# A decoder's last stage: gated squares in a new order, and identity products at four borders

## The reference

```python
shared = x2 @ sw1.T * _sqrelu(x2 @ swg.T) @ sw2.T      # x2: 2048 tokens x 256
xl = x2 @ Wdown.T                                       # 2048 x 64
...                                                     # w_dense: 2048 x 16, the gates, 8 of 16 not zero
for e in range(E):                                      # E = 16
    ye = xl @ rw1[e].T * _sqrelu(xl @ rwg[e].T) @ rw2[e].T
    acc = acc + w_dense[:, e:e + 1] * ye
out = shared + acc @ Wup.T
```

## Time and profile before

| what | value |
|---|---|
| median of 3 runs | 1069.51 us (1068.92 to 1071.56) |
| the profiled execution, its time | 1066.24 us |
| its span | 1064.5 us |
| mean granted clock | 0.977 |
| DVE, ACT, POOL busy | 778.5, 710.1, 303.4 us |
| last stage begins, experts' pairs begin, last of them ends | about 916.8, 949.7, 1047.25 us |

### The profile page before, as it was taken

How to read it: one execution, slowest core, us unless ns; L and a number is a source line. 1 busy time by engine, 2 the same in 40 slices (tenths; PEclk the granted TensorE clock), 3 DMA queues, 4 the chain that set the end, 5 groups by cost and what they waited for, 6 DMA issues and landing times. The chain is left out here.

```text
span 1064.5 us, 19092 instructions
## 1 busy us (share of the span) xinstructions
PE 999.2 (94%) x6751; PEld 830.1 (78%) x6751; DVE 778.5 (73%) x1541; ACT 710.1 (67%) x1961; POOL 303.4 (28%) x250
## 2 busy tenths in 40 slices
PE   7999999999999999999988867899998799799998
PEld 3888988988998898898987655677776699575555
DVE  5888868667676676766767888899887444567775
ACT  5888777767767777766743366678787244458882
POOL 1342333332332233333300110244454000103442
PEclk9999999999999999999999898899999899899999
DMA  7221000000000000000241000000000000024432
GB/s 214 85 61 59 2 1 1 2 1 1 1 1 2 1 23 14 1 1 2 80 123 22 1 1 1 1 2 2 2 2 2 2 1 2 16 66 121 101 99 80
DMA packets 31837, 31.79 MB, mean 30 GB/s; under 512 B 8192, under 2 KB 23296, under 8 KB 31744
## 3 DMA queue, kind: packets, MB, share of 16 engines
q1 hardware_dynamic: 31744, 30.59, 10.3%
...
## 5 line engine op out<-in xcount | busy, mean ns | idle before, releaser
L345 POOL TENSOR_TENSOR roped_q<-roped_q,sin_q 128x512 f32<-128x512 f32 x64 | 82.0, 1281 | 301.1 <-DVE sin_q L490 301.1
L1622 ACT ACTIVATE win_P<-banks,win_neg_max 128x128 f32<-128x128 f32 x256 | 91.3, 380 | 27.6 <-DVE win_neg_max L1696 26.8
L345 POOL TENSOR_TENSOR roped_k<-roped_k,sin_k 128x512 f32<-128x512 f32 x64 | 83.3, 1301 | 46.1 <-DVE sin_k L490 46.1
L399 ACT ACTIVATE P<-banks,neg_max 128x128 f32<-128x128 f32 x256 | 90.5, 372 | 5.8 <-DVE neg_max L515 5.6
L433 ACT ACTIVATE oT_hi<-banks,bv_col 128x512 fp32r<-128x512 f32 x64 | 44.1, 689 | 74.2 <-PE banks L663 74.2
L1578 POOL TENSOR_TENSOR win_P<-win_P,win_inv 128x512 f32<-128x512 f32 x64 | 66.9, 1046 | 72.9 <-DVE win_inv L1701 72.9
L408 ACT ACTIVATE sin_k<-banks 64x512 f32<-64x512 f32 x128 | 76.0, 594 | 11.0 <-PE banks L37 9.4
L518 DVE SCALAR_TENSOR_TENSOR oT_lo<-banks,bv_col,oT_hi 128x512 fp32r<-128x512 f32 x64 | 47.9, 749 | 42.6 <-ACT oT_hi L433 42.0
L408 ACT ACTIVATE sin_q<-banks 64x512 f32<-64x512 f32 x128 | 76.0, 594 | 2.9 <-PE banks L37 0.7
L625 PE MATMUL banks<-WO_lo,oT_hi 128*128 128x256 f32 x256 | 72.9, 285 | 0.0
L489 DVE SCALAR_TENSOR_TENSOR roped_k<-banks,qk_bias,cos 128x512 f32<-128x512 f32 x64 | 48.0, 750 | 32.6 <-ACT sin_k L408 32.6
...
## 6 DMA issues: line engine op xcount, KB each, us to landing
...
```

Source lines behind the costliest of these rows:

```text
L345: nc.gpsimd.tensor_tensor(roped[w][:, p, :], roped[w][:, p, :], sin_part[w][:], ALU.add).then_inc(roped_sum[w], 1)
L399: ins = nc.scalar.activation(P[:, i, :], SC[:, i * 128:(i + 1) * 128], ACT.Exp, bias=neg_max[:, r % 2, i:i + 1], accum_out=exp_sum[:, r % ...
L1622: ins = nc.scalar.activation(P[:, h % 2, s, i, :], SC[2 * (h % 2) + s][:, i * 128:(i + 1) * 128], ACT.Exp, bias=neg_max[:, h % 2, at:at + ...
```

## The change

In `phase_moe`:

- The latent is kept once, `XL_hi` and `XL_lo`, two groups in the two halves of the partitions (`split_latent`). `up_pair(n)` makes the gate products of two steps and then their up products: for each, three products of 64 rows (high x low, low x high, high x high) for either half in turn, into two banks. `U1` has four banks, `Y` two.
- ScalarE makes two relus, then two squares; `relu` and `squared` have four slots.
- The gates multiply the square, not the output of `down`: on GpSimd for three of four steps, on VectorE (`gate_here`) for the one with s % 4 == 1. `gate_of` holds all 2048 tokens of an expert on all 128 partitions, loaded in two halves of tokens.
- `down(n)` adds up over the experts in `Y[n % 2]` in PSUM and comes two pairs after its up product; `weigh` and the additions are gone. At the end ScalarE and VectorE copy the two sums to `acc`.
- `split_latent(3)` and `gate_hidden(0)` come after the gates, whose transpose on TensorE comes before the up product of step 2.

At four borders, `keep_busy(count)` and a loop add products of the identity with itself, 128 columns of float32, into a bank that nobody reads: 16 in the retention, 7 before the spline stage's transposes, 6 and 5 at the start of cross attention, 5 at its end, 5 and 2 in the last stage.

```diff
                 pe.wait_ge(gate_ready, 2 * PAIRS)
                 pe.wait_ge(w_split, 2)
+                def keep_busy(count):
+                    for _ in range(count):
+                        nc.tensor.matmul(WOB[0][:, 0:128], ident[:], ident[:], start=True, stop=True)
+                keep_busy(16)
                 for p in range(PAIRS + 1):
                     if p < PAIRS:
                         transpose_wy(p)
...
             def _(pe):
+                def keep_busy(count):
+                    for _ in range(count):
+                        nc.tensor.matmul(bank[4][:, 0:128], ident[:], ident[:], start=True, stop=True)
+                keep_busy(7)
...
+                def keep_busy(count):
+                    for _ in range(count):
+                        nc.tensor.matmul(OUT[:, 0:128], ident[:], ident[:], start=True, stop=True)
+                keep_busy(6)
                 transpose_x(0)
+                keep_busy(5)
                 project_q(0)
                 project_k(0)
                 transpose_x(1)
...
                     weigh(2 * i + 1)
+                for _ in range(5):
+                    nc.tensor.matmul(KB[:, 0:128], ident[:], ident[:], start=True, stop=True)
...
-        weighted = spare[:].rearrange("p b h n -> p (b h n)")[:, 0:3 * GW].rearrange("p (i n) -> p i n", i=3)
-        acc = spare[:].rearrange("p b h n -> p (b h n)")[:, 3 * GW:5 * GW].rearrange("p (i n) -> p i n", i=2)
+        acc = sb("moe_acc", [128, 2, GW])
...
-        UG, U1, Y = bank[0:2], bank[2:5], (bank[6], bank[7], bank[5])
-        up_bank = lambda s: Y[1] if s == 0 else U1[s % 3]
+        UG, U1, Y = bank[0:2], bank[2:6], bank[6:8]
+        up_bank = lambda s: Y[0] if s == 0 else U1[s % 4]
...
+        on_dve = lambda s: s % 4 == 1
+        gated_by_dve = lambda s: max(0, (s + 3) // 4 - 1)
+        gated_by_pool = lambda s: max(0, s + 1 - NG - gated_by_dve(s))
+        pair_done = lambda s: s + 1 if s < NG else NG + (s - NG) // 2 + 1
...
                     if e >= GATE_SLOTS:
-                        sp.wait_ge(weighted_done, 2 * (e - GATE_SLOTS) + 2)
-                    row = gate_rows[e].rearrange("(c h n) -> h c n", c=2, h=2)
-                    for half in range(2):
-                        src = row[half].rearrange("(a c) n -> a c n", a=1).broadcast_to([LAT, 2, GW])
-                        sp.dma_start(gate_of[half * LAT:(half + 1) * LAT, e % GATE_SLOTS], src).then_inc(gate_loaded[e % GATE_SLOTS], 16)
+                        sp.wait_ge(pool_gated, gated_by_pool(NG * (e - GATE_SLOTS + 2) - 1))
+                        sp.wait_ge(dve_gated, e - GATE_SLOTS + 1)
+                    src = gate_rows[e].rearrange("(a n) -> a n", a=1).broadcast_to([128, B * S])
+                    for c in range(2):
+                        cols = slice(c * 2 * GW, (c + 1) * 2 * GW)
+                        sp.dma_start(gate_of[e % GATE_SLOTS][:, cols], src[:, cols]).then_inc(gate_loaded[2 * (e % GATE_SLOTS) + c], 16)
...
-                for n in range(2, HALVES):
-                    pool.wait_ge(weighted_done, n + 1)
-                    wait(pool, acc_added, n - 3)
-                    nc.gpsimd.tensor_tensor(acc[:, n % 2], acc[:, n % 2], weighted[:, n % 3], ALU.add).then_inc(acc_added, 1)
+                for s in range(NG, STEPS):
+                    if on_dve(s):
+                        continue
+                    e, g = s // NG - 1, s % NG
+                    pool.wait_ge(gate_loaded[2 * (e % GATE_SLOTS) + g // 2], 16 * (e // GATE_SLOTS + 1))
+                    pool.wait_ge(square_done, s + 1)
+                    nc.gpsimd.tensor_tensor(squared[:, s % 4, :], squared[:, s % 4, :], gate_of[e % GATE_SLOTS][:, g * GW:(g + 1) * GW], ALU.mult).then_inc(pool_gated, 1)
...
+                    rows = slice(g % 2 * LAT, (g % 2 + 1) * LAT)
                     act.wait_ge(lat_projected, g + 1)
-                    wait(act, XL_ready, g - 1)
-                    nc.scalar.activation(lat_hi[:, g % 2], LAT_BANKS[g % 3], ACT.Copy).then_inc(lat_rounded, 1)
-                def square_relu(s):
-                    act.wait_ge(gate_ups_done, s + 1)
-                    wait(act, square_done, s - 1)
-                    nc.scalar.activation(relu[:, s % 2, :], UG[s % 2], ACT.Relu).then_inc(relu_done, 1)
+                    nc.scalar.activation(XL_hi[rows, g // 2, :], LAT_BANKS[g % 3][rows, :], ACT.Copy).then_inc(lat_rounded, 1)
+                def rectify(s):
+                    act.wait_ge(gate_ups_done, pair_done(s))
+                    wait(act, square_done, s - 3)
+                    nc.scalar.activation(relu[:, s % 4, :], UG[s % 2], ACT.Relu).then_inc(relu_done, 1)
+                def square(s):
                     act.wait_ge(relu_done, s + 1)
-                    wait(act, hidden_done, s - 1)
-                    nc.scalar.activation(squared[:, s % 2, :], relu[:, s % 2, :], ACT.Square).then_inc(square_done, 1)
+                    wait(act, hidden_done, s - 3)
+                    nc.scalar.activation(squared[:, s % 4, :], relu[:, s % 4, :], ACT.Square).then_inc(square_done, 1)
...
+                for n in range(HALVES):
+                    if n % 2 == 0 and n // 2 + 1 < E_:
+                        round_expert(n // 2 + 1)
+                    for s in (NG + 2 * n, NG + 2 * n + 1):
+                        rectify(s)
+                    for s in (NG + 2 * n, NG + 2 * n + 1):
+                        square(s)
+                act.wait_ge(downs_done, HALVES - 1)
+                nc.scalar.activation(acc[:, 0], Y[0], ACT.Copy).then_inc(acc_ready[0], 1)
...
-                def mix_latent(g):
+                def split_latent(g):
+                    rows = slice(g % 2 * LAT, (g % 2 + 1) * LAT)
                     dve.wait_ge(lat_rounded, g + 1)
-                    STT(XL[:, g, :], lat_hi[:, g % 2].bitcast(F32), low_rows[:, 0:1], LAT_BANKS[g % 3], ALU.mult, ALU.add).then_inc(XL_ready, 1)
+                    TT(XL_lo[rows, g // 2, :], LAT_BANKS[g % 3][rows, :], XL_hi[rows, g // 2, :].bitcast(F32), ALU.subtract).then_inc(XL_ready, 1)
+                def gate_here(s):
+                    e, g = s // NG - 1, s % NG
+                    dve.wait_ge(gate_loaded[2 * (e % GATE_SLOTS) + g // 2], 16 * (e // GATE_SLOTS + 1))
+                    dve.wait_ge(square_done, s + 1)
+                    TT(squared[:, s % 4, :], squared[:, s % 4, :], gate_of[e % GATE_SLOTS][:, g * GW:(g + 1) * GW], ALU.mult).then_inc(dve_gated, 1)
                 def gate_hidden(s):
-                    dve.wait_ge(ups_done, s + 1)
-                    dve.wait_ge(square_done, s + 1)
+                    dve.wait_ge(ups_done, pair_done(s))
+                    if s < NG:
+                        dve.wait_ge(square_done, s + 1)
+                    elif on_dve(s):
+                        dve.wait_ge(dve_gated, gated_by_dve(s))
+                    else:
+                        dve.wait_ge(pool_gated, gated_by_pool(s))
                     if s < NG:
                         dst = shared[:, s, :]
                     else:
                         wait(dve, downs_done, (s - NG - 6) // 2 + 1)
                         dst = hidden[:, s % 6, :]
-                    TT(dst, up_bank(s), squared[:, s % 2, :], ALU.mult).then_inc(hidden_done, 1)
+                    TT(dst, up_bank(s), squared[:, s % 4, :], ALU.mult).then_inc(hidden_done, 1)
...
-                def weigh(n):
-                    e, c = n // 2, n % 2
-                    dve.wait_ge(downs_done, n + 1)
-                    if c == 0:
-                        dve.wait_ge(gate_loaded[e % GATE_SLOTS], 32 * (e // GATE_SLOTS + 1))
-                    wait(dve, acc_added, n - 4)
-                    dst = acc[:, c] if e == 0 else weighted[:, n % 3]
-                    TT(dst, Y[n % 3], gate_of[:, e % GATE_SLOTS, c, :], ALU.mult).then_inc(weighted_done, 1)
...
-                mix_latent(3)
...
-                gate_hidden(0)
...
                 TT(gates_by_expert[:].rearrange("p e g i -> p i g e"), gates[:].rearrange("p (i g) e -> p i g e", g=NG),
                    gate_sum[:, 1, :].rearrange("p (i g a) -> p i g a", g=NG, a=1).broadcast_to([128, GROUP, NG, E_]), ALU.mult).then_inc(gates_ready, 1)
+                split_latent(3)
+                gate_hidden(0)
+                gate_hidden(1)
                 split_expert(0)
-                for s in range(1, STEPS):
+                for s in range(2, NG):
                     gate_hidden(s)
-                    e, g = EXPERT(s)
-                    if g == 1 and 0 <= e and e + 1 < E_:
-                        split_expert(e + 1)
-                    n = (s - 8) // 2
-                    if s % 2 == 0 and n >= 0:
-                        weigh(n)
-                for n in range((STEPS - 9) // 2 + 1, HALVES):
-                    weigh(n)
+                for n in range(HALVES):
+                    s = NG + 2 * n
+                    if n % 2 == 0 and n // 2 + 1 < E_:
+                        split_expert(n // 2 + 1)
```

(62 more changed lines are left out.)

60 lines of the change are left out of this document (23 added, 37 removed).

## The result

The changed kernel took 1060.57 us in the median (1057.05 to 1061.06, four runs) against 1069.89 of the kernel before beside it (1068.92 to 1071.56). The ratio is 0.9904, interval 0.9879 to 0.9929. The forecast was 1055.5 with a range of 1049 to 1066: faster, and by 9 us in place of 14. The profiled execution took 1060.81 us, with a span of 1059.0 against 1064.5.

What follows compares the result with a forecast made beforehand. TensorE, busy 94% of the span, was taken as the bound, with half-clock stretches at four borders. Experts -7.6 us and borders -6.4 made -14.0: 1052.2 profiled, 1055.5 as median, range 1049 to 1066.

Steps and rivals of the forecast that it cites:

- Expert products: Experts' stage: 64-row products run side by side on two row halves; a pair falls from 3.07 to 2.65 us, saving 13.4.
- Rival B: Experts' stage: the row halves of the new products don't overlap; fully in series +30 us, total 1093; chance 0.06.
- The chain: Experts' stage: relus, squares, gate and hidden products take 5.5 us, making the pair period 2.72; costs 2.2 us.
- rival A: Experts' stage: the chain through GpSimd sets the pace, period 3.05 us; total 1066.1; chance 0.16.
- Fill and drain: Experts' stage: down products two pairs late; TensorE stands 2.6 us at the start and waits some 1.0 at the end.
- Gates by DMA: Experts' stage: larger gate loads at 339 GB/s stay hidden; expert 3's weights land at 963, wanted at 963.9; no cost.
- rival D: Experts' stage: gate broadcasts keep to 231 GB/s, so weights land late; +6 us, total 1061.5; chance 0.08.
- Borders: Identity products hold the clock at four borders: retention 1.7, spline 0.4, cross attention 2.5, last stage 1.8; 6.4 us saved.
- six from 836.0 end at 837.3: Start of cross attention: six identity products end 0.4 us after the old transposes' start; part of a 2.5 us border gain.
- Rival C: Four borders: the identity products don't hold the clock; 0 instead of -6.4 us, total 1061.9; chance 0.10.
- Carrying over the 3.3 us: Whole kernel: the median stays 3.3 us above the profiled execution, turning 1052.2 into 1055.5.

Runs made afterwards that it cites:

- four_slots: Changed kernel with four buffers of expert weights instead of three, later loads ordered gates then weights: 1055.99 us, ratio 0.9873 to the kernel before.
- window_end: Changed kernel with five more identity products at the end of the window stage, before its last twelve products: 1056.76 us, ratio 0.9881 to the kernel before.
- the repeated halves: Changed kernel without its identity products, ratio 0.9955 to the kernel before; and the kernel before with only the identity products added, ratio 0.9959.

## Why the prediction was right in sign and 5 us too low

- **Expert products: right, and mis-sized a little.** Two halves at once, 0.23 us a two. TensorE's own pair is 2.60 us, not 2.65: 32 x 0.47 = 15.0 us given back, not 13.4. Rival B was out on sounder grounds than I gave, since not even the order matters.
- **The chain: right.** A period of 2.74 against 2.72. Over TensorE's own 2.60 it adds 0.14 us a pair, 3.8 us over 27 pairs (2.73, so 3.5, in `four_slots`), where I had 2.2. VectorE's SBUF product took 0.675 us (forecast 0.66), so rival A, in which each of them waits out a GpSimd product, fell. That is in part the timing: between 995.42 and 996.10 it runs in a stand of GpSimd, which starts at 996.14, so no run shows its price beside a GpSimd product that began first. The port showed in two other places: the split at 0.946 (0.42 without gate products), and three of GpSimd's 48 products, which took 1.47 to 1.67 us against a median of 1.29, each while a VectorE operation with two SBUF inputs that had begun just before it was running. The Trainium skill's "SBUF — State Buffer", section "SBUF: two separate sides", says that whichever of two such operations starts first holds the shared port pair to its end, and the other waits. The trace agrees, in both directions: here GpSimd's operations waited as well as VectorE's.
- **Fill and drain: right together.** `four_slots`, where no transfer is late by more than 0.46 us, gives 114.5 - 106.5 = 8.0. From 15.0 less 3.5 to 8.0 there are 3.5 us for both; I had 3.6. In the changed kernel the up product that needs the first pair's hidden tiles starts 6.3 us after the stage's first product (955.07, forecast 6.2).
- **Gates by DMA, "Free": this step failed.** The rate was about what I took or more (401 and 333 GB/s in the two windows shown below and 371 from 950.00 to 963.28, against 339), so rival D's mechanism, slow broadcasts, was wrong: a wait like its own came by another way. By the Trainium skill, "SBUF — State Buffer", section "Door 1: The DMA port swizzle", partitions 0 to 63 reach only half of the SBUF ports. The trace agrees: these rates of loads to 128 partitions stand beside 231 for the old loads to 64. What failed, first, is the time at which ScalarE wants expert 3's weights. I had 0.7 + 2.6 + 4 x 2.72 = 14.2 us after the first product, but down products run two pairs late, so the first two pairs have none and are 1.2 us shorter each. That is 11.8, and `four_slots` shows 11.2. Second, the weights came at 14.5 (forecast 13.3): from the first gate load at 946.99 to 963.28 the transfers moved 331 GB/s, 5.4 MB, where I had counted 4.33. The difference has the size of one more expert's gates (1.05 MB, issued at 956.61, before the weights had landed); that these held up the weights is not shown. The wait costs 3.7 us by `four_slots` against the changed kernel's profile. This is more than the stage's shortfall: -7.6 forecast, -4.3 measured, -8.0 without the wait. The two windows, of the changed kernel:

```profile
950.00:952.00 2.00, 1.52 (x14) 0.91 (x12) 0.00 (x0) 1.99 (x5) 0.47 (x1) 1.00 1.04 401
...
962.00:964.00 2.00, 0.25 (x2) 0.00 (x0) 0.96 (x2) 0.72 (x2) 0.25 (x1) 1.00 1.06 333
```

- **Borders: retention and the last stage right, cross attention wrong; the spline border is too small to tell.** Retention -2.1 (forecast -1.7), spline -0.2 (-0.4; the runs differ by 1), the last stage -1.9 (-1.8), cross attention -0.1 (-2.5). The step that failed there is "six from 836.0 end at 837.3". They began where I had put them, with the stage's first normalised tile (836.86 here, 836.08 before), but the clock had already fallen in the window stage's last stand, and they took 2.90 us in place of 1.3. I had priced this ("If a clock has already fallen when they start, each takes twice as long") but left it out of the sum. The trace of before could have told me: its last products of the window stage, behind that stand, already start 0.22 us apart, where the same products with the full clock start 0.12 apart (`window_end`).

```profile
831.31 0.58 PE L35 MATMUL banks<-win_w_lo,win_oT_hi 128*128 128x256 f32 x1 [1.44 <-DVE win_oT_lo L1710]
831.68 0.42 PE L36 MATMUL banks<-win_w_hi,win_oT_lo 128*128 128x256 f32 x1
831.90 0.42 PE L37 MATMUL banks<-win_w_hi,win_oT_hi 128*128 128x256 f32 x1
```

- **Rival C** came true at one border of four. The clock also fell in the window stage, which is 2.3 us longer in this profile than before. Twelve profiles of kernels with identity products have 171.8 to 175.8 us there, two without have 173.3, and the clock differs in the same way (0.75 to 0.93, and 0.87). That the identity products of earlier stages make the clock fall there is possible, and not shown.
- **Carrying over the 3.3 us** between the profiled execution and the median was wrong. The changed kernel's profiled execution took 1060.81 us and its median is 1060.57; that of before was a fast one of its kind. By the profiled executions alone the change gave 5.4 us, by the medians 9.3, and the repeated halves side with the medians.
